# A gated cross-attention and feed-forward block on one core: the order of all five instruction streams is rewritten, the matmul stages run column by column, and the context chunks and weight sums change places

## The chip, the cores and the metric

The kernel runs on one core of a Trainium2 chip. The metric is the device time in microseconds (us) of one execution; lower is better. TensorE (PE) multiplies matrices, VectorE (DVE), ScalarE (ACT) and GpSimd (POOL) work on elements, and SyncE (SP) issues nearly all transfers (DMA). Each engine works through its own instructions in order and waits on semaphores where it needs another one's result.

## What is computed

```python
# x (2, 1024, 2048), ctx (2, 2048, 2048), weight (2048, 2048), all f32
def fake_quant(x, scale, zp):
    q = jnp.clip(jnp.round(x / s + z), 0, 255)
    return (q - z) * s
def xattn(x1, x2):                  # x1 = _layernorm(x), x2 = ctx
    return jnp.matmul(fake_quant(x1, ...), fake_quant(x2, ...))
def ffn(x, weight):                 # x = _layernorm(x)
    s = QP / jnp.clip(jnp.max(jnp.abs(x), axis=-1, keepdims=True), 1e-05, None)
    xq = jnp.clip(jnp.round(x * s), QN, QP) / s
    scale_w = 1.0 / jnp.clip(jnp.mean(jnp.abs(weight)), EPS, None)
    tw = jnp.clip(jnp.round(weight * scale_w), -1.0, 1.0)
    return jnp.einsum('bsi,oi->bso', xq, tw) / scale_w
x = x + jnp.tanh(g_xattn[0]) * xattn(_layernorm(x), ctx_4096)
x = x + jnp.tanh(g_ffn[0]) * ffn(_layernorm(x), weight)
```

Two things matter for the order. The feed-forward part needs the mean of all absolute weights before it can quantise the first one, so the weights are read twice. And each row of the first result must be complete before its layernorm and its largest value are known.

## The kernel before, in words

There are two batches `b` of 8 row tiles `m` (128 rows each) and 4 column chunks `c` (512 columns). A **unit** is one accumulator bank: one tile `m` times one chunk `c`, 16 matmuls of 128x512. TensorE does 128 units in four stages: X0 and X1 (cross-attention of batch 0 and 1), F0 and F1 (feed-forward of batch 0 and 1); stage X0 is units 0 to 31, X1 32 to 63, F0 64 to 95, F1 96 to 127. `UNITS` is their order. After a unit DVE adds it into the f32 rows `h` (`add`), which frees the bank (`acc_free`). X0 rotates over 8 banks, the later stages over 4, since the other 4 hold the halves that `halve` (ACT) writes and `max_h` (DVE) reduces to find each row's maximum.

Before a tile can be multiplied it goes through a chain: load x, statistics on DVE (`stats_x`), a square root on ACT (`deviation1`), `scale_x` on DVE, quantisation to int8 on POOL (`quant1`), a transposing transfer (`turn`, issued by SP), and a cast to bf16 into `lhs` (`lhs_bf`). `lhs` holds 8 tiles only, so a tile of the next stage can be cast when the last unit of the same `m` of this stage is done. `stats_h`, `scale_h`, `halve`, `max_h`, `peak_h`, `quant2` are the same chain for the feed-forward part.

A context chunk comes in 8 pieces of 512 KB: load, quantise to int8 (`ctx_quant`, mostly POOL), cast to bf16 (`ctx_bf`, ACT). Batch 0's pieces go through 8 slots (`stage`); batch 1's pieces and all weight halves go through `ring`, 4 slots of 512 KB, in the order of the table `RING` ("ctx" a piece of batch 1's context, "sum" a half weight tile for the mean, "quant" the same half again for quantisation). `q2` has two places for a bf16 chunk. Before, batch 0's chunks 2 and 3 are put into `upper`, the space of batch 1's tiles 4 to 7 in `h`. Later `q2` holds the ternary weights `tw`.

Everything is ordered by hand: the calls in each engine's function are that engine's order. SP's order also fixes the order of the transfers; a `turn` whose int8 tile is not ready holds up all loads behind it. `pace` lets a load start only when the one some three sizes before it has landed.

Of the kernel before, what the change touches and what calls it, by code (L numbers as in the profile page):

```python
# [5 lines left out]
def flamingo_gated_block(nc, x, ctx, g_xattn, g_ffn, s1, z1, s2, z2, weight, out):  # L6
# [8 lines left out]
    P = 128  # L15
# [13 lines left out]
    AHEAD = 3  # L29
# [28 lines left out]
    TURNS += [("h", 0, m) for m in A] + [("w", 0, t) for t in range(2 * TPC)]  # L58
    TURNS += [("h", 0, m) for m in Z] + [("w", 0, t) for t in range(2 * TPC, WT)] + [("h", 1, m) for m in range(M)]
# [22 lines left out]
    LN1 = [(0, m, m + 1) for m in range(M)] + [(1, 0, 4), (1, 4, 6), (1, 6, 8)]  # L82
    LN2 = [(b, h, h + NB) for b in range(B) for h in (0, NB)]
    LN2_VAR, LN2_OPS, PEAK_OPS = 2 * NB + 1, 2 * NB + 6, 4

    def ln1_count(g, whole):

        sizes = [m1 - m0 for _, m0, m1 in LN1]
        steps = [2 * n + 1 + (5 if n == 1 else 7) for n in sizes]
        return sum(steps[:g]) + (steps[g] if whole else 2 * sizes[g] + 1)  # L90

    def group_of(groups, b, m):
        return next(g for g, (gb, m0, m1) in enumerate(groups) if gb == b and m0 <= m < m1)
# [7 lines left out]
    with es:  # L101
# [16 lines left out]
        upper = h[:, 1, NB:M, :].rearrange("p m d -> p (m d)").bitcast(bf16).rearrange("p (c k n) -> p c k n", c=2, k=K)  # L118
# [3 lines left out]
        def chunk(b, c):  # L122
            return q2[:, c % 2, :, :] if b == 1 or c < 2 else upper[:, c - 2, :, :]
# [99 lines left out]
        def _(sp):  # L223
# [97 lines left out]
            for m in A[1:]:  # L321
                load_x(1, m)
# [663 lines left out]
```

## Time and profile before

| | us |
|---|---|
| median of 3 runs (lowest, highest) | 550.48 (550.24, 551.34) |
| the profiled execution | 551.01 |
| its span, first to last instruction | 549.2 |
| TensorE busy in the span | 466.0 |
| DVE, ACT, POOL busy | 255.2, 232.6, 160.9 |
| mean granted TensorE clock | 0.95 of full speed |
| read from memory, written | 83.89 MB, 16.78 MB |

The span is 1.8 us shorter than the time of the same execution. TensorE is the engine that is busy most; its idle time stands in a few places, so the way to read this profile is along TensorE's time line, asking at each gap what it waited for and what that in turn waited for.

### The profile page before, as it was taken

What the parts mean: (1) busy time and instruction counts of PE and PEld (TensorE: products, weight loads), DVE (VectorE), ACT (ScalarE), POOL (GpSimd) and SP (SyncE); (2) the same over time, 40 slices, a digit from 0 to 9 for tenths busy, and PEclk for the clock granted to TensorE, in tenths of its full rate; (3) what the DMA queues carried; (4) which work ended last, traced back from release to release, by engine and by line L of the source; (5) the groups of instructions that cost most, each with busy time, mean ns of one, the idle gap of its engine ahead of it and who ended that gap; (6) DMA issues with size and microseconds to landing.
All of it is one profiled execution on the core that took longest, in us unless ns stands there. A gap on an engine that the chain in (4) does not pass through costs nothing.

```text
span 549.2 us, 5796 instructions
## 1 busy us (share of the span) xinstructions
PE 466.0 (85%) x2027; PEld 202.2 (37%) x2048; DVE 255.2 (46%) x455; ACT 232.6 (42%) x235; POOL 160.9 (29%) x122
## 2 busy tenths in 40 slices
PE   0179968989994896759899779974999999999997
PEld 0024423434441342314344334431444444444443
DVE  4732152768107963793633374937932222222221
ACT  1266645221783567847974446238631410000000
POOL 2537653213962200177211471210431100000000
PEclk9999998999996898959999889996999999999999
DMA  7969968675999888788989998982180803030322
GB/s 243 261 199 338 326 205 287 187 222 205 267 366 344 226 251 294 245 280 200 333 263 268 272 208 229 305 230 81 76 222 9 229 1 154 0 154 0 154 76 76
DMA packets 88293, 113.78 MB, mean 207 GB/s; under 512 B 54720, under 2 KB 54720, under 8 KB 88256
## 3 DMA queue, kind: packets, MB, share of 16 engines
q1 hardware_dynamic: 87392, 113.27, 68.5%
q8 instruction: 25, 0.41, 0.3%
q10 hardware_dynamic: 864, 0.00, 0.1%
q14 instruction: 12, 0.10, 0.0%
HBM read 83.89 MB, written 16.78 MB: 183 GB/s over the span
## 4 chain that ended last, share of the span: by engine, by line
PE 31%; issue 30%; POOL 15%; DMA 12%; ACT 6%; DVE 3%; SPq 3%; POOLq 0%; ACTq 0%; DVEq 0%
PE acc L725 31%; POOL ctx_i L407 10%; DMA ring<-in_L_ffn_weight 5%; POOL tile_i L389 3%; DMA turned_i<-tile_i 3%; SPq L287 2%; DMA ctx_i<-tile_i 2%; ACT acc L521 1%; POOL tile_i L416 1%; ACT q L499 1%; DMA h<-in_ctx 1%; ACT ring L537 1%; DMA h<-in_x 1%; ACT q L554 1%; ACT tile_i L546 1%
## 5 line engine op out<-in xcount | busy, mean ns | idle before, releaser
L725 PE MATMUL acc<-q,lhs 128*128 128x512 fp8e4 x1024 | 226.6, 385 | 16.6 <-DVE h L851 11.0
L671 PE MATMUL acc<-q,lhs 128*128 128x512 bf16 x753 | 182.9, 400 | 56.2 <-DVE lhs L833 25.0
L851 DVE SCALAR_TENSOR_TENSOR h<-acc,smalls,h 128x512 f32<-128x512 f32 x128 | 93.8, 748 | 152.6 <-PE acc L725 121.3
L725 PEld LDWEIGHTS acc<-q,lhs 128*128 128x128 bf16 x1024 | 101.2, 99 | 142.0 <-DVE h L851 14.8
L671 PEld LDWEIGHTS acc<-q,lhs 128*128 128x128 bf16 x768 | 75.7, 101 | 162.4 <-issue 41.6
L389 POOL TENSOR_SCALAR tile_i<-h,smalls 128x2048 int8<-128x2048 f32 x32 | 68.4, 2141 | 120.5 <-DVE smalls L785 38.1
L760 DVE BATCH_NORM_STATS2 smalls<-h 128x6 f32<-128x512 f32 x64 | 39.8, 681 | 55.7 <-DMA h<-in_x 55.6
L671 PE MATMUL acc<-h,lhs 128*128 128x512 bf16 x250 | 57.5, 387 | 6.7 <-ACT h L499 6.4
L499 ACT ACTIVATE q<-ctx_i 128x1024 bf16<-128x1024 int8 x48 | 49.6, 1052 | 26.9 <-POOL ctx_i L407 26.0
L530 ACT ACTIVATE lhs<-turned_i 128x2048 bf16<-128x2048 int8 x20 | 37.9, 1902 | 46.7 <-DMA turned_i<-tile_i 46.7
L407 POOL TENSOR_SCALAR ctx_i<-ring,smalls 128x1024 int8<-128x1024 f32 x32 | 38.1, 1195 | 51.1 <-DMA ring<-in_ctx 48.7
L816 DVE TENSOR_REDUCE smalls<-acc 128x1 f32<-128x1024 f32 x32 | 37.7, 1220 | 18.9 <-ACT acc L521 18.7
L407 POOL TENSOR_SCALAR ctx_i<-h,smalls 128x1024 int8<-128x1024 f32 x28 | 33.4, 1195 | 26.4 <-DMA h<-in_ctx 25.6
L671 PEld LDWEIGHTS acc<-h,lhs 128*128 128x128 bf16 x256 | 25.3, 100 | 38.4 <-ACT h L499 7.3
L796 DVE BATCH_NORM_STATS2 smalls<-h 128x6 f32<-128x512 f32 x64 | 39.4, 679 | 0.0
L521 ACT ACTIVATE acc<-h,smalls 128x1024 f32<-128x1024 f32 x32 | 37.3, 1194 | 4.6 <-DVE smalls L816 4.6
L416 POOL TENSOR_SCALAR tile_i<-ring,smalls 128x1024 int8<-128x1024 f32 x16 | 18.9, 1182 | 59.0 <-DMA ring<-in_L_ffn_weight 51.2
L537 ACT ACTIVATE ring<-ring 128x1024 f32<-128x1024 f32 x32 | 33.4, 1045 | 6.2 <-DMA ring<-in_L_ffn_weight 6.1
L546 ACT ACTIVATE tile_i<-ring,smalls 128x1024 int8<-128x1024 f32 x16 | 18.1, 1144 | 33.8 <-DMA ring<-in_L_ffn_weight 33.6
L506 ACT ACTIVATE smalls<-smalls 128x1 f32<-128x1 f32 (+2 forms) x11 | 2.2, 200 | 49.1 <-DVE smalls L765 49.1
L499 ACT ACTIVATE h<-ctx_i 128x1024 bf16<-128x1024 int8 x16 | 16.8, 1054 | 8.5 <-POOL ctx_i L407 8.5
L530 ACT ACTIVATE lhs<-ctx_i 128x2048 bf16<-128x2048 int8 x8 | 15.1, 1902 | 4.2 <-DMA ctx_i<-tile_i 4.2
(57 smaller groups left out, 82.8 us busy)
## 6 DMA issues: line engine op xcount, KB each, us to landing
ring<-in_L_ffn_weight SPq DMA_DIRECT2D x64, 512.0 KB, 5.6
h<-in_ctx SPq DMA_DIRECT2D x32, 512.0 KB, 6.3
ring<-in_ctx SPq DMA_DIRECT2D x32, 512.0 KB, 6.0
h<-in_x SPq DMA_DIRECT2D x30, 512.0 KB, 6.6
out<-h SPq DMA_DIRECT2D x28, 512.0 KB, 2.6
out<-h SPq DMA_DIRECT2D x8, 256.0 KB, 2.4
h<-in_x SPq DMA_DIRECT2D x4, 256.0 KB, 5.0
turned_i<-tile_i SPq DMA_TRANSPOSE x32, 4.6
```

The source lines that it names most:

```text
L389: nc.gpsimd.tensor_scalar(tile_i8[:, n % TP, :], tile, scale, offset, ALU.mult, ALU.add).then_inc(i8_ready[n % TP], 1)
L407: nc.gpsimd.tensor_scalar(ctx_i8[:, piece % NB, :], src, inv_s[:, 1:2], dz[:, 1:2], ALU.mult, ALU.add).then_inc(used, 1)
L499: nc.scalar.activation(flat(chunk(b, c)[:, p * KP:(p + 1) * KP, :]), ctx_i8[:, piece % NB, :], ACT.Copy).then_inc(ctx_ready, 1)
L521: nc.scalar.activation(spare[:, cols], h[:, b, m, cols], ACT.Identity, bias=nb2[:, t:t + 1], scale=hr2[:, t:t + 1]).then_inc(half_ln, 1)
L530: nc.scalar.activation(in_pairs(lhs[:, m, :, :]), pairs_apart(n), ACT.Copy).then_inc(lhs_act, 1)
L537: nc.scalar.activation(half, half, ACT.Abs, accum_out=w_part[:, n:n + 1]).then_inc(ring_used[i % NB], 1)
L671: done = nc.tensor.matmul(acc, lhs[:, m, k, :], chunk(b, c)[:, k, :], start=(k == 0), stop=(k == K - 1))
L725: done = nc.tensor.matmul(psum[:, bank(u), :], lhs[:, m, k, :], tw[:, c, k, :], start=(k == 0), stop=(k == K - 1))
L760: ins = V.bn_stats(s[:, 6 * c:6 * c + 6], h[:, b, m, c * NC:(c + 1) * NC])
L796: ins = V.bn_stats(s[:, 6 * c:6 * c + 6], h[:, b, m, c * NC:(c + 1) * NC])
L816: V.tensor_reduce(amax[:, t, s:s + 1], spare[:, s * PW:(s + 1) * PW], AX.X, ALU.max, apply_absolute_value=True).then_inc(half_max, 1)
L851: V.scalar_tensor_tensor(out=hc, in0=psum[:, bank(u), :], scalar=gain, in1=hc, op0=ALU.mult, op1=ALU.add).then_inc(acc_free, 1)
```

## The change

- **Units.** X0 ran the upper four tiles (A) through all four chunks, then the lower four (Z). Now A and Z both run through chunks 0 to 2, and chunk 3 is done last for all eight tiles. X1, F0 and F1 ran in pairs of columns, half by half; now each column is done for all eight tiles before the next.
- **Places.** Batch 0's chunk 3 goes where chunk 0 was (`q2`), so `upper` holds one chunk and tiles 6 and 7 of batch 1 are free from the start. `chunk_before` names the column whose end a chunk has to wait for. The ternary weights of chunk `c` lie at `(c + 2) % C`.
- **Ring.** The weight sums stand between batch 1's context chunks; the last context chunk now comes after all sums.
- **Orders.** The call lists of SP, POOL, ACT, DVE and the opening of PE are all rewritten. A row tile's statistics of batch 1 are scaled one by one, those of the feed-forward part two by two (before in fours). Batch 1's tiles 0 to 3 are cast on DVE, no longer on ACT. The transposes of the feed-forward tiles 4 to 7 stand after the fourth weight tile's, no longer after the eighth's. `pace` allows one more load ahead after the first 24.

```diff
-    AHEAD = 3
-    OPENING = [(m, c) for c in range(C) for m in A]
-    OPENING += [(NB, c) for c in range(C)] + [(m, c) for c in range(C) for m in Z[1:]]
-    PAIRS = [(m, c) for pair in ((0, 1), (2, 3)) for half in (A, Z) for c in pair for m in half]
-    UNITS = [(X0, m, c) for m, c in OPENING] + [(s, m, c) for s in (X1, F0, F1) for m, c in PAIRS]
+    OPENING = [(m, c) for half in (A, Z) for c in range(C - 1) for m in half] + [(m, C - 1) for m in range(M)]
+    BY_COLUMN = [(m, c) for c in range(C) for m in range(M)]
+    UNITS = [(X0, m, c) for m, c in OPENING] + [(s, m, c) for s in (X1, F0, F1) for m, c in BY_COLUMN]
...
-    TURNS += [("h", 0, m) for m in A] + [("w", 0, t) for t in range(2 * TPC)]
-    TURNS += [("h", 0, m) for m in Z] + [("w", 0, t) for t in range(2 * TPC, WT)] + [("h", 1, m) for m in range(M)]
+    TURNS += [("h", 0, m) for m in A] + [("w", 0, t) for t in range(TPC)]
+    TURNS += [("h", 0, m) for m in Z] + [("w", 0, t) for t in range(TPC, WT)] + [("h", 1, m) for m in range(M)]
...
-        return (kind == "x" and b == 0 and m < NB) or (kind == "w" and m % 2 == 0)
+        return (kind == "x" and m < NB) or (kind == "w" and m % 2 == 0)
...
-    SUM_FIRST = 24
-    RING = [("ctx", i) for i in range(2 * PIECES)] + [("sum", i) for i in range(SUM_FIRST)]
-    RING += [("ctx", i) for i in range(2 * PIECES, C * PIECES)] + [("sum", i) for i in range(SUM_FIRST, 2 * WT)]
-    RING += [("quant", i) for i in range(2 * WT)]
+    RING = [("ctx", i) for i in range(PIECES)] + [("sum", n) for n in range(6)]
+    RING += [("ctx", i) for i in range(PIECES, 2 * PIECES)] + [("sum", n) for n in range(6, 20)]
+    RING += [("ctx", i) for i in range(2 * PIECES, 3 * PIECES)] + [("sum", n) for n in range(20, 2 * WT)]
+    RING += [("ctx", i) for i in range(3 * PIECES, C * PIECES)] + [("quant", n) for n in range(2 * WT)]
...
         def chunk(b, c):
-            return q2[:, c % 2, :, :] if b == 1 or c < 2 else upper[:, c - 2, :, :]
+            return q2[:, 1 - c % 2, :, :] if b else upper if c == 2 else q2[:, int(c == 1), :, :]
+
+        def chunk_before(b, c):
+
+            return {(0, 3): (X0, 0), (1, 0): (X0, 1), (1, 1): (X0, 3), (1, 2): (X1, 0), (1, 3): (X1, 1)}.get((b, c))
+
+        def ternary(c):
+            return tw[:, (c + 2) % C, :, :]
...
-                behind = 0
+                behind, far = 0, 3 if len(loads) < 24 else 4
...
-                    else:
-                        sp.wait_ge(acc_done, units_end(X0, c=2 + (m - NB) // 2))
+                    elif m < NB + 2:
+                        sp.wait_ge(acc_done, units_end(X0, c=2))
```

Three places show what the new orders do. First SP, in the stretch from the transposes of batch 1's tiles 4 to 7 to the last context chunk; before, it reads (`turned_i<-tile_i` is a transpose, `ring<-in_ctx` a context piece, `ring<-in_L_ffn_weight` a weight half, `h<-in_x` half an x tile):

```order
L246 DMA h<-in_x 128x1024 x4
L274 DMA ring<-in_L_ffn_weight 128x1024 x2
L287 DMA_TRANSPOSE turned_i<-tile_i 128x8x128 x2
L274 DMA ring<-in_L_ffn_weight 128x1024 x4
L287 DMA_TRANSPOSE turned_i<-tile_i 128x8x128
L274 DMA ring<-in_L_ffn_weight 128x1024 x2
L287 DMA_TRANSPOSE turned_i<-tile_i 128x8x128
L274 DMA ring<-in_L_ffn_weight 128x1024 x12
L268 DMA ring<-in_ctx 128x2x512 x16
```

The same stretch of SP in the changed kernel:

```order
L270 DMA ring<-in_ctx 128x2x512 x6
L286 DMA_TRANSPOSE turned_i<-tile_i 128x8x128
L270 DMA ring<-in_ctx 128x2x512
L273 DMA ring<-in_L_ffn_weight 128x1024 x3
L286 DMA_TRANSPOSE turned_i<-tile_i 128x8x128 x2
L273 DMA ring<-in_L_ffn_weight 128x1024 x4
L286 DMA_TRANSPOSE turned_i<-tile_i 128x8x128
L273 DMA ring<-in_L_ffn_weight 128x1024 x7
L270 DMA ring<-in_ctx 128x2x512 x8
L273 DMA ring<-in_L_ffn_weight 128x1024 x12
L270 DMA ring<-in_ctx 128x2x512 x3
```

The x loads are gone from here, the 16 context pieces in one run are split into 8 and 8, and the 12 sums that stood ahead of them or behind them now stand between.

Second DVE, at the casts of the last two ternary weight tiles of DVE (`q<-`), in F0. Before (`h<-acc,smalls,h` is an `add`):

```order
L798 BN_AGGR smalls<-smalls 128x2
L851 SCALAR_TENSOR_TENSOR h<-acc,smalls,h 128x512
L840 TENSOR_SCALAR q<-turned_i 128x16x128
L840 TENSOR_SCALAR q<-ctx_i 128x16x128
L803 TENSOR_SCALAR smalls<-smalls 128x4
L805 RECIPROCAL smalls<-smalls 128x4
```

The last of these two casts in the changed kernel, with what stands around it:

```order
L1057 SCALAR_TENSOR_TENSOR h<-acc,smalls,h 128x512
L1022 TENSOR_REDUCE smalls<-acc 128x1
L1046 TENSOR_SCALAR q<-ctx_i 128x16x128
L1057 SCALAR_TENSOR_TENSOR h<-acc,smalls,h 128x512
L1022 TENSOR_REDUCE smalls<-acc 128x1
```

Before, both casts stand together behind the add of unit 75; now the first stands behind that of unit 78 and the last behind that of unit 81, with adds and reductions between them.

Third ACT, in X1 from the square roots of batch 0's second layernorm on. Before (`q<-ctx_i` is `ctx_bf`, `acc<-h,smalls` half a tile's `halve`, `ring,smalls<-ring` a weight sum):

```order
L510 ACTIVATE smalls<-smalls 128x4
L537 ACTIVATE ring,smalls<-ring 128x1024 x2
L521 ACTIVATE acc<-h,smalls 128x1024 x2
L537 ACTIVATE ring,smalls<-ring 128x1024 x2
L521 ACTIVATE acc<-h,smalls 128x1024 x2
L537 ACTIVATE ring,smalls<-ring 128x1024 x2
L521 ACTIVATE acc<-h,smalls 128x1024 x2
L537 ACTIVATE ring,smalls<-ring 128x1024 x2
L521 ACTIVATE acc<-h,smalls 128x1024 x2
L499 ACTIVATE q<-ctx_i 128x1024 x8
```

The changed kernel, from the same point on:

```order
L615 ACTIVATE smalls<-smalls 128x2 x3
L604 ACTIVATE q<-ctx_i 128x1024 x2
L625 ACTIVATE acc<-h,smalls 128x1024
L604 ACTIVATE q<-ctx_i 128x1024 x2
L625 ACTIVATE acc<-h,smalls 128x1024
L604 ACTIVATE q<-ctx_i 128x1024 x3
L625 ACTIVATE acc<-h,smalls 128x1024
L641 ACTIVATE ring,smalls<-ring 128x1024 x4
L604 ACTIVATE q<-ctx_i 128x1024
L641 ACTIVATE ring,smalls<-ring 128x1024 x4
L625 ACTIVATE acc<-h,smalls 128x1024
```

Four whole tiles stood in one block between sums, ahead of all 8 casts of chunk 2; now the halves are spread among the casts of chunk 2 and the sums.

## Rows read from the trace of the kernel before

**Rows 1.** The page: span, TensorE's busy time, its granted clock in 40 slices.

```profile
span 549.2 us, 5796 instructions
...
PE 466.0 (85%) x2027; PEld 202.2 (37%) x2048; DVE 255.2 (46%) x455; ACT 232.6 (42%) x235; POOL 160.9 (29%) x122
...
PEclk9999998999996898959999889996999999999999
```

**Rows 2.** The waits of TensorE: waiter, releaser, total us, times, longest.

```profile
PE acc L671 <- DVE lhs L833: 25.0, 2, 18.2
PE acc L671 <- DVE h L851: 18.2, 9, 6.8
PE acc L725 <- DVE h L851: 11.0, 1, 11.0
PE acc L671 <- ACT q L499: 10.2, 12, 2.2
```

**Rows 3.** TensorE's time line: start, length, instructions, idle before and its releaser.

```profile
46.52 13.99 PE L671 MATMUL acc<-q,lhs 128*128 128x512 bf16 x63 [0.42 <-ACT q L499]
...
153.73 13.98 PE L671 MATMUL acc<-q,lhs 128*128 128x512 bf16 x62
174.52 9.78 PE L671 MATMUL acc<-q,lhs 128*128 128x512 bf16 x31 [6.82 <-DVE h L851]
...
305.06 15.66 PE L725 MATMUL acc<-q,lhs 128*128 128x512 fp8e4 x64 [2.79 <-ACT q L554]
323.53 43.20 PE L725 MATMUL acc<-q,lhs 128*128 128x512 fp8e4 x192 [2.81 <-ACT q L554]
377.76 167.72 PE L725 MATMUL acc<-q,lhs 128*128 128x512 fp8e4 x768 [11.04 <-DVE h L851]
```

**Rows 4.** DVE's time line at two of those gaps.

```profile
164.63 2.47 DVE L760 BATCH_NORM_STATS2 smalls<-h 128x6 f32<-128x512 f32 x4 [16.86 <-DMA h<-in_x]
...
278.16 0.21 DVE L865 TENSOR_SCALAR smalls<-smalls 128x1 f32<-128x1 f32 x1
...
368.09 1.29 DVE L840 TENSOR_SCALAR q<-ctx_i 128x2048 fp8e4<-128x2048 int8 x1 [6.36 <-DMA ctx_i<-tile_i]
```

**Rows 5.** SP's time line: runs of loads and some transposes.

```profile
36.67 24.84 SPq L255 DMA_DIRECT2D h<-in_ctx  x17
...
196.78 22.78 SPq L274 DMA_DIRECT2D ring<-in_L_ffn_weight  x12
222.51 30.70 SPq L268 DMA_DIRECT2D ring<-in_ctx  x16
...
273.33 3.78 SPq L274 DMA_DIRECT2D ring<-in_L_ffn_weight  x4
...
296.17 1.23 SPq L287 DMA_TRANSPOSE ctx_i<-tile_i  x1
...
314.16 1.35 SPq L287 DMA_TRANSPOSE ctx_i<-tile_i  x1
...
317.19 6.35 SPq L287 DMA_TRANSPOSE turned_i<-tile_i  x2
323.63 4.49 SPq L287 DMA_TRANSPOSE ctx_i<-tile_i  x2
...
359.63 1.25 SPq L274 DMA_DIRECT2D ring<-in_L_ffn_weight  x2
```

**Rows 6.** The page's DMA issues: count, size, median us to landing.

```profile
ring<-in_ctx SPq DMA_DIRECT2D x32, 512.0 KB, 6.0
...
turned_i<-tile_i SPq DMA_TRANSPOSE x32, 4.6
```

**Rows 7.** Groups by line and form: busy us, mean ns | idle before.

```profile
L407 POOL TENSOR_SCALAR ctx_i<-ring,smalls 128x1024 int8<-128x1024 f32 x32 | 38.1, 1195 | 51.1 <-DMA ring<-in_ctx 48.7 <-ACT q L499 1.5
...
L833 DVE CAST lhs<-turned_i 128x2048 bf16<-128x2048 int8 x4 | 5.1, 1275 | 7.0 <-DMA turned_i<-tile_i 6.9
...
L781 DVE SCALAR_TENSOR_TENSOR smalls<-smalls 128x1 f32<-128x1 f32 x8 | 1.8, 220 | 0.3
```

More of the change, by code:

```diff
@@ L233, in pace, with load_x0 @@
                 loads.append((landing, value, size))
+            def load_x0(first, end):
+                for c in range(first, end):
+                    pace(x0_in[c], 16, 0.5)
+                    sp.dma_start(h[:, 0, 0, c * NC:(c + 1) * NC], x_t[0][:, c * NC:(c + 1) * NC]).then_inc(x0_in[c], 16)
             def load_x(b, m):
@@ new lines, in _ @@
+            half_sum(6, 9)
+            lhs_bf(TURN_X[1, 5])
+            lhs_bf(TURN_X[1, 6])
+            half_sum(9, 13)
+            lhs_bf(TURN_X[1, 7])
+            half_sum(13, 17)
+            ctx_bf(47, 48)
+            half_sum(17, 20)
+            deviation2(0, 0)
+            deviation2(0, 2)
+            deviation2(0, 4)
+            ctx_bf(48, 50)
+            halve(0, 0, 0)
+            ctx_bf(50, 52)
+            halve(0, 0, 1)
+            ctx_bf(52, 55)
+            halve(0, 1, 0)
@@ new lines, in _ @@
+            half_sum(20, 24)
+            ctx_bf(55, 56)
+            half_sum(24, 28)
+            halve(0, 1, 1)
+            half_sum(28, 32)
+            halve(0, 2, 0)
+            halve(0, 2, 1)
+            deviation2(0, 6)
+            ctx_bf(56, 57)
+            halve(0, 3, 0)
+            ctx_bf(57, 59)
+            halve(0, 3, 1)
+            halve(0, 4, 0)
+            ctx_bf(59, 60)
+            halve(0, 4, 1)
+            ctx_bf(60, 62)
+            halve(0, 5, 0)
+            halve(0, 5, 1)
@@ L679, in pieces_ready, with opening @@
                 pe.wait_ge(ctx_ready, b * FIRST + c * PIECES + p + 1)
-            def opening(m, first, end):
+            def opening(m, c, first, end):
                 for p in range(first, end):
-                    pieces_ready(0, 0, p)
+                    pieces_ready(0, c, p)
                     if p == 0:
-                        begin(unit(X0, m, 0), TURN_X[0, m])
-                    xattn(0, m, 0, piece_of(p))
-            for p in range(4):
-                opening(0, p, p + 1)
-                opening(1, p, p + 1)
@@ new lines, in _ @@
+            opening(0, 3, 0, 8)
+            opening(1, 3, 0, 8)
+            opening(2, 3, 0, 8)
+            opening(3, 3, 0, 8)
+            opening(4, 3, 0, 8)
+            opening(5, 3, 0, 8)
+            opening(6, 3, 0, 8)
+            opening(7, 3, 0, 8)
+            for c in range(C):
+                for m in range(M):
+                    begin(unit(X1, m, c), TURN_X[1, m])
+                    for p in range(PIECES):
+                        if m == 0:
+                            pieces_ready(1, c, p)
+                        xattn(1, m, c, piece_of(p))
@@ L857, in weight_sum @@
                 for j in range(NB):
-                    dve.wait_ge(ring_used[j], RING_AT["quant", 0] // NB)
+                    i = max(i for i, (what, n) in enumerate(RING) if what == "sum" and i % NB == j)
+                    dve.wait_ge(ring_used[j], i // NB + 1)
                 step(n_w, w_steps, V.tensor_reduce(w_sum[:, :], w_part[:, :], AX.X, ALU.add))
```

1022 lines of the change are left out of this document (639 added, 383 removed).

## The prediction

> **What bounds the kernel now.** I read the page first. TensorE is busy for 466.0 of 549.2 us and its granted clock falls in several slices [rows 1]. The work itself is fixed: 2048 matmuls; a long undisturbed run of 768 takes 167.72 us, 0.2184 us each, so a unit of 16 costs 3.5 us, a stage of 32 units some 111 and a column of 8 units 27.8 [rows 3]. Then its waits [rows 2]: 25.0 us for the first tiles' casts at the start, 18.2 and 11.0 for banks that DVE frees, 10.2 for context casts. Then its time line, gap by gap [rows 3], and behind each gap the engine that released it.
>
> The start is a loading phase: the matmuls run without gaps from 46.5 on. X0 ends at 153.7. X1 should end 111 us later, at 265, and ends at 302.3 (305.06 - 2.79). One cause is the gap of 6.82: DVE stood 16.86 us before the statistics of a batch 1 tile [rows 4], because tiles 4 to 7 lie in `upper` and can't be loaded until X0's last columns are done, and the adds are queued behind them. Others are the four tiles that DVE reduces in one block, and chunk 2, whose place in `q2` comes free only 4 units before it is needed. F0 loses 2.79 and 2.81 to weights, then 11.04 because DVE stands before its last two weight casts (the last at 368.09) with the adds queued behind [rows 4]. After each of these gaps a run is too long for its count: 64 matmuls in 15.66 us are 1.7 over the 13.98 of a run at full clock (153.73). From 377.76 on nothing is lost; the last matmul ends at 545.5 and the span 3.7 later.
>
> **The change, stage by stage.** I follow the new orders with durations of the old trace.
>
> *Start and X0.* The first tile's cast moves behind the statistics of the fourth x tile, and POOL's quantisation of tile 1 behind a context piece, so the first matmul comes some 5 us later. That costs little: the fourth tile is cast at about the same time as before, since its load has the same bytes ahead of it, and the eight open banks let TensorE catch up. Then loads flow as in the run of 17 pieces in 24.84 us, 1.46 us each [rows 5]. Chunk 0 is complete on SP only after 14 pieces, no longer after 8, so I put its end on TensorE at 48; the 8 units of the upper tiles' chunks 1 and 2 take 28, 76, and 1 for single pieces: 77. Their last piece has the four lower x tiles (worth 8 pieces) and 10 pieces between it and chunk 0's last, which lands at some 44: 44 + 18 x 1.46 = 70, and is no hindrance. The lower tiles' casts hang on where SP issues their transposes: tile 7's stands behind pieces 24 to 31, the last issued at about 70 + 8 x 1.46 = 81, then 4.6 for the transpose [rows 6] and some 2 for the cast: 88. The same count gives 69, 77 and 83 for tiles 4 to 6, and the units need them at 77, 81, 85 and 93, in the order in which PE's opening is written. Chunk 3 needs column 0 to be done (about 97), takes 8 casts, and is ready by 107, needed at 118. So the remaining 20 units run on: 77 + 20 x 3.5 = 147. X0 gains about 7 us on 153.7.
>
> *X1.* Tiles 6 and 7 are loaded before 100, 4 and 5 at 118 (column 2 of X0 done), so DVE has its statistics well ahead: the 6.82 goes, with the 2.8 by which the run after it is too long (9.78 for some 32 matmuls of 0.218). Each chunk's place comes free a full column ahead instead of 4 units: that removes the 10.2 for context casts but for remnants. TensorE alone would end X1 at 147 + 111 = 258. What then comes last is the ring. Item 22 reuses the slot of a piece of chunk 1, and those wait for X0's end, so it goes out at about 150; 41 more must follow until the last context piece, which is now behind all sums. A ring item took 22.78 / 12 = 1.90 and 30.70 / 16 = 1.92 us in two runs of different kind [rows 5]. Both fit 4 slots that are each held for a landing of 6.0 and a conversion of 1.195 [rows 6, 7], (6.0 + 1.2) / 4 = 1.8. So 41 x 1.92 = 79, plus five transposes that SP issues in between at some 1.25 each and about 2 of waiting for them, 8: issued at 237, landed at 243, cast at 246. The seven tiles after the first follow: 246 + 7 x 3.5 = 270.5 for X1's end, 32 us earlier than now.
>
> *F0's start.* Before, the weight scale was known at 278.4 [rows 4] and F0 began at 305.06, 27 later, through quantising, transposing and casting four weight tiles. In the new order the sums are over before the last context chunk, so the scale is not waited for; the first weight half lands one ring item after the last context piece, at 245, and 245 + 2 for its neighbour + 27 = 274. That is a little later than X1's end, so F0 starts at 274 instead of 305.
>
> *Inside F0.* Now column 1's weights come after the transposes of tiles 4 to 7. From the fourth weight transpose (296.17) to the eighth (314.16) 18 us passed, and the four tile transposes took 317.19 to 328.1, 11 [rows 5]. From a fourth weight transpose to the stage that needs it are 305.06 - 296.17 = 9. So column 1 is ready 18 + 11 = 29 us after column 0, and needed 27.8 after: I charge 3 us, with the half clock after it. Columns 2 and 3 are 18 to 22 apart (32 halves in 87.5 us from 273.33 to 360.9 are 2.7 each [rows 5], 22 a column) and needed 27.8 apart: hidden. The last weight cast on DVE began at 368.09, 95 us after the first weight loads were issued at 273.33 [rows 4, 5]. Counted from 239, one ring item after the last context piece, this is 334; it stands before the add of unit 82 now, and TensorE can reach unit 86 without that add, at 274 + 22 x 3.5 = 351. The 11.04 goes.
>
> *More instructions.* Layernorm steps in pairs or singly instead of fours add some 64 small DVE operations, at up to 0.22 each about 14 us in all, and four casts of 1.275 move to DVE [rows 7], which is busy for 255.2 of 549.2 us [rows 1]. I cost them at nothing: they lie beside TensorE's units, of which each leaves DVE 3.5 us for an add. With that cover gone the most is 14 + 5 = 19; nothing is gained by them on DVE, and ACT is relieved of four casts.
>
> **Sum.** 274 (F0 starts) + 3 + 64 units x 3.5 = 223.6 + 3.7 (end) = 504.3. I add 4 for one more short gap with the lengthened run behind it, of the size that both edges of F0 show now, since no order of five queues fits everywhere: span 508. The profiled execution's time is 1.8 above its span, and the median 0.5 below that execution: 509.5.
>
> **A rule of the skill.** In the run of 17 pieces 512 KB took 1.46 us, which is 359 GB/s [rows 5]. The Trainium skill, "DMA: Bandwidth & Descriptors", section "Where 436 GB/s comes from", gives some 358 GB/s for a core as the memory side's limit; by that the trace agrees that this run was at the limit and the ring, at 273 GB/s, is not. If the limit and not the slots set the ring's pace, the sum would be that of the first rival.
>
> **Rivals.**
> - *The ring runs at the stage's rate* (more loads are let ahead, and slots are freed sooner by the spread order): 1.46 instead of 1.92, 42 x 0.46 = 19 earlier. Then TensorE itself is last, X1 ends at 258, F0 starts there: 258 + 3 + 223.6 + 3.7 = 488, 490 as a time. Against it: `pace` was not what the 1.92 fits, four slots are. 10%.
> - *The ring runs at 2.7 us an item*, as in the weight phase, because ACT and POOL now have halves, casts and quantisations between the ring's items and in-order engines hold slots: 42 x 0.78 = 33 later, 537 span, 539; with half of it 522. For it: ACT's new order has a halve behind every few ring items, and each waits for DVE's reduction. 22%.
> - *Slower than before.* One loop decides: DVE's adds 49 and 50 stand behind reductions whose halves stand on ACT behind sums 20 to 31, which wait for ring slots; POOL converts the last context pieces only behind quantisations that need those reductions. If each side waits for the other at most items, an item costs more than 1.92 + (549 - 508) / 42 = 2.90 us, and the kernel is slower than now. Nothing in the trace has an item that slow over 42 in a row: 4%.
> - *The order moves waits about and the sum stays*: 1% within 0.2%.
>
> The forecast, 496 to 520, has 63%. The range should leave out 2 in 10: it reaches down to 494, into the first rival, and up to 530, over the half-slow ring. 0.2%, about 1.1 us, is what a measurement of this kernel can tell from no change. Faster 0.95, same 0.01, slower 0.04.
>
> **What would show it.** Right: TensorE without a gap over 2 us from about 46 to 205; no wait of DVE for x over 5 us after 110; `ctx_bf` of the last chunk 1.9 us apart with POOL waiting for the ring; F0 starting within 5 us of X1's end, near 274; from there no gap over 3 us. Wrong: ring items over 2.3 us apart with the slot held by ACT or DVE; TensorE waiting for adds in X1; the lower tiles' transposes late on SP around 80 to 95, which would move everything behind by as much.

## The result and the profile after

The changed kernel takes 503.25 us (median of 4, 502.31 to 504.25) against 550.36 (549.05 to 551.34): a ratio of 0.915, with a 95% interval of 0.912 to 0.917. The forecast was 509.5, in a range of 494 to 530. In a second group of runs, on which the first comparisons below rest, the same kernel took 502.22, a ratio of 0.915 (0.908 to 0.923).

The page of the changed kernel, in answer to [rows 1]:

```profile
span 500.5 us, 5951 instructions
...
PE 450.2 (90%) x2048; PEld 200.3 (40%) x2048; DVE 290.2 (58%) x523; ACT 226.3 (45%) x241; POOL 163.4 (33%) x121
...
PEclk9999999999999999998599999999999999999999
```

Of the dents in the granted clock one is left, in slices 19 and 20 (225 to 250 us). TensorE's time line, in answer to [rows 3]:

```profile
28.82 7.41 PE L836 MATMUL acc<-q,lhs 128*128 128x512 bf16 x24 [28.82 <-ACT q L604]
37.73 8.79 PE L836 MATMUL acc<-q,lhs 128*128 128x512 bf16 x40 [1.50 <-DVE lhs L1039]
...
116.42 38.15 PE L836 MATMUL acc<-q,lhs 128*128 128x512 bf16 x176
...
171.78 58.87 PE L836 MATMUL acc<-q,lhs 128*128 128x512 bf16 x272 [0.69 <-ACT lhs L634]
234.14 2.62 PE L836 MATMUL acc<-q,lhs 128*128 128x512 bf16 x6 [3.49 <-DVE h L1057]
241.93 1.03 PE L836 MATMUL acc<-q,lhs 128*128 128x512 bf16 x2 [5.17 <-ACT q L604]
244.00 1.98 PE L836 MATMUL acc<-q,lhs 128*128 128x512 bf16 x4 [1.04 <-ACT q L604]
248.16 26.82 PE L836 MATMUL acc<-q,lhs 128*128 128x512 bf16 x116 [2.17 <-ACT q L604]
275.61 221.17 PE L942 MATMUL acc<-q,lhs 128*128 128x512 fp8e4 x1024 [0.63 <-DVE h L1057]
```

X0's last 8 units begin at 116.4 and end 27.7 later, at 144.1. F0 and F1 are one line: 1024 matmuls in 221.17 us without a gap. The whole saving can be laid along three stretches:

| stretch of the span | before | after | saved |
|---|---|---|---|
| start to the end of X0 | 153.7 | 144.1 | 9.6 |
| X1 with what follows it, to F0's start | 151.3 | 131.5 | 19.8 |
| F0's start to the last matmul | 240.4 | 221.2 | 19.2 |

The last matmul's distance to the end, 3.7, is the same. What still costs time is one place: 11.9 us in four gaps between 230.6 and 248.2. The table of windows shows it and the clock around it (length of the window; busy times of PE, PEld, DVE, ACT and POOL; then granted clock, the DMA engines' share and GB/s):

```profile
205.00:222.00 17.00, 17.00 (x80) 7.74 (x79) 6.64 (x12) 13.55 (x22) 6.47 (x4) 1.00 0.92 278
222.00:242.00 20.00, 11.35 (x48) 4.52 (x46) 7.60 (x19) 6.40 (x7) 4.02 (x5) 0.81 0.39 126
242.00:275.00 33.00, 29.77 (x122) 11.86 (x122) 28.93 (x42) 26.51 (x21) 17.95 (x12) 0.86 1.07 271
275.00:497.00 222.00, 221.17 (x1024) 100.12 (x1024) 100.30 (x154) 65.69 (x51) 34.81 (x22) 1.00 0.50 148
```

From 222 to 242 TensorE, ACT and POOL are busy for a smaller share than in the window above, and the DMA share falls to 0.39, so neither bandwidth nor a busy engine explains it. POOL's time line does:

```profile
222.68 1.22 POOL L471 TENSOR_SCALAR ctx_i<-ring,smalls 128x1024 int8<-128x1024 f32 x1 [0.78 <-DMA ring<-in_ctx]
232.26 0.40 POOL L501 PARTITION_ALL_REDUCE smalls<-smalls  x1 [8.36 <-issue]
239.60 3.54 POOL L471 TENSOR_SCALAR ctx_i<-ring,smalls 128x1024 int8<-128x1024 f32 x3 [6.94 <-issue]
```

The all-reduce that adds the weight sums over the partitions takes 0.40 us. But POOL does nothing for 8.36 us ahead of it and 6.94 behind it, and the releaser is "issue": it waited for nothing that the profile shows. From 223.9 to 239.6 POOL converts no context piece. Around it ACT waits 13.60 for the next piece (`240.82 ... ACT L604`), DVE 7.87 for the scale, with the adds behind, and SP needs 18.63 us for the last four context pieces, since their slots aren't freed. The prediction did not have this.

### The profile page after: what moved, and what is told of

Read it like the earlier page. It is cut to its first block, busy times and chain, and to the rows that moved or that the text cites. A ratio compares the mean times of both kernels' runs of the same rounds, so it can differ in the third digit from the quotient of the medians.

```text
span 500.5 us, 5951 instructions
## 1 busy us (share of the span) xinstructions
PE 450.2 (90%) x2048; PEld 200.3 (40%) x2048; DVE 290.2 (58%) x523; ACT 226.3 (45%) x241; POOL 163.4 (33%) x121
## 4 chain that ended last, share of the span: by engine, by line
PE 67%; issue 15%; POOL 6%; DMA 4%; ACT 4%; DVE 2%; SPq 1%; POOLq 0%; ACTq 0%; DVEq 0%
PE acc L942 44%; PE acc L836 22%; POOL ctx_i L471 5%; DMA h<-in_ctx 3%; ACT q L604 2%; DMA h<-in_x 2%; POOL tile_i L453 1%; DVE q L1046 1%; DVE smalls L1000 0%; ACT acc L625 0%; DVE h L1057 0%; SPq L236 0%; DVE smalls L992 0%; ACT L610 0%; ACT L582 0%
## 5 line engine op out<-in xcount | busy, mean ns | idle before, releaser
L836 PE MATMUL acc<-q,lhs 128*128 128x512 bf16 x896 | 201.8, 387 | 45.9 <-ACT q L604 37.8
L942 PE MATMUL acc<-q,lhs 128*128 128x512 fp8e4 x1024 | 221.2, 379 | 0.6 <-DVE h L1057 0.6
L836 PEld LDWEIGHTS acc<-q,lhs 128*128 128x128 bf16 x896 | 87.7, 99 | 159.2 <-ACT q L604 43.5
L942 PEld LDWEIGHTS acc<-q,lhs 128*128 128x128 bf16 x1024 | 100.1, 98 | 121.7 <-DVE h L1057 1.1
L604 ACT ACTIVATE q<-ctx_i 128x1024 bf16<-128x1024 int8 x56 | 56.7, 1047 | 50.1 <-POOL ctx_i L471 39.6
L471 POOL TENSOR_SCALAR ctx_i<-ring,smalls 128x1024 int8<-128x1024 f32 x32 | 40.1, 1256 | 41.9 <-DMA ring<-in_ctx 33.6
L634 ACT ACTIVATE lhs<-turned_i 128x2048 bf16<-128x2048 int8 x16 | 30.2, 1901 | 37.1 <-PE acc L942 24.9
L836 PE MATMUL acc<-h,lhs 128*128 128x512 bf16 x128 | 28.0, 379 | 0.0
L836 PEld LDWEIGHTS acc<-h,lhs 128*128 128x128 bf16 x128 | 12.5, 98 | 15.1
L1039 DVE CAST lhs<-turned_i 128x2048 bf16<-128x2048 int8 x8 | 11.4, 1430 | 4.9 <-DMA turned_i<-tile_i 4.7
L604 ACT ACTIVATE h<-ctx_i 128x1024 bf16<-128x1024 int8 x8 | 8.4, 1052 | 5.7 <-POOL ctx_i L471 5.4
```

The costliest lines, as they stand in the source:

```text
L471: nc.gpsimd.tensor_scalar(ctx_i8[:, piece % NB, :], src, inv_s[:, 1:2], dz[:, 1:2], ALU.mult, ALU.add).then_inc(used, 1)
L604: nc.scalar.activation(flat(chunk(b, c)[:, p * KP:(p + 1) * KP, :]), ctx_i8[:, piece % NB, :], ACT.Copy).then_inc(ctx_ready, 1)
L634: nc.scalar.activation(in_pairs(lhs[:, m, :, :]), pairs_apart(n), ACT.Copy).then_inc(lhs_act, 1)
L836: done = nc.tensor.matmul(acc, lhs[:, m, k, :], chunk(b, c)[:, k, :], start=(k == 0), stop=(k == K - 1))
L942: done = nc.tensor.matmul(psum[:, bank(u), :], lhs[:, m, k, :], ternary(c)[:, k, :], start=(k == 0), stop=(k == K - 1))
```

## The experiments

Twelve kernels ran, in three groups of four; each group is compared with the kernel before on the same chip (549.3, 550.3 and 550.9 us). `one` is a column of ones. The first four are about POOL's stall; the first of them is the changed kernel again, with no edit.

> The changed kernel once more, as the ruler for the three runs beside it on the same chip. Both theories: 502 to 505 us; TensorE stands four times between 230 and 250 us, 11 to 12 us in all, and POOL does nothing that the profile shows for 8 us before and 7 us after its sum over the partitions.

**Measured:** 502.22 us, span 500.3. The result repeats, with four gaps of together 12.1 us and F0's start at 275.39.

**The sum over the partitions on TensorE** in place of POOL:

```diff
-            weights_over_partitions()
...
+                    if unit(X1, m, c) == 55:
+                        pe.wait_ge(w_steps, 1)
...
+                        nc.tensor.matmul(psum[:, bank(55), 0:1], one[:, :].to_broadcast([P, P]), w_sum[:, :],
+                                         start=True, stop=True).then_inc(w_all_done, 1)
+                        pe.wait_ge(w_steps, 2)
```

(The memset of `one` and the wait for it are left out here. TensorE goes on when DVE has read the sum, and `weight_scale` stands ahead of one reduction more in DVE's order.)

> The sum of the weight sums over the partitions is made by one small f32 matmul on TensorE, ahead of unit 55, instead of POOL's sum over the partitions. Theory S (the switch of POOL to that operation and back, some 15 us, holds the last five context pieces): POOL converts the last context pieces without a break, the four gaps of TensorE near 240 shrink from 12 us to 1 to 3, F0 starts at 262 to 267 instead of 275.6, and the time is 489 to 494 us. Theory R (the ring and its loads would have held the last context pieces anyway): the last context piece lands at the same time, 501 to 504 us.

**Measured:** 490.47 us (490.27 to 492.93), ratio 0.894 (0.887 to 0.902), span 488.5. TensorE's time line of this kernel from the new matmul on:

```profile
225.20 0.28 PE L929 MATMUL acc<-smalls 128*128 128x1 f32 x2
225.73 5.35 PE L833 MATMUL acc<-q,lhs 128*128 128x512 bf16 x24 [0.25 <-DVE smalls L1073]
231.80 0.60 PE L833 MATMUL acc<-q,lhs 128*128 128x512 bf16 x2 [0.71 <-ACT q L601]
...
235.95 27.77 PE L833 MATMUL acc<-q,lhs 128*128 128x512 bf16 x116 [2.60 <-ACT q L601]
263.56 221.18 PE L945 MATMUL acc<-q,lhs 128*128 128x512 fp8e4 x1024
```

The sum is there in 0.28 us, 3.9 us of gaps are left of 11.9 (one of 0.34 is not in the rows), and F0 starts at 263.56 instead of 275.61: those 12.05 us are the whole difference of the two spans. This version beats both kernels.

**The all-reduce late**, behind the last context piece on POOL (the scale in DVE's order behind it), the computation otherwise as in the changed kernel:

```diff
-            ctx_quant(56, 59)
-            weights_over_partitions()
-            ctx_quant(59, 62)
+            ctx_quant(56, 62)
             quant2(0, 2)
             ctx_quant(62, 64)
+            weights_over_partitions()
```

> POOL's sum over the partitions stays, but stands behind the last context piece, and DVE's scale of the weights behind the add of unit 56. Theory S: the context gaps go (last context cast near 240 instead of 249), but the scale is known near 250 instead of 233 and the weights of F0's first column are late: F0 starts at 272 to 280 with a wait for weights or adds ahead of it, 499 to 508 us. Theory R: nothing gained at the context pieces, and the late scale costs up to 10 us: 505 to 513.

**Measured:** 503.69 us (501.85 to 505.07). The stall moves with the instruction and costs as much at F0's start:

```profile
243.85 0.40 POOL L501 PARTITION_ALL_REDUCE smalls<-smalls  x1 [8.76 <-issue]
251.57 2.04 POOL L453 TENSOR_SCALAR tile_i<-h,smalls 128x2048 int8<-128x2048 f32 x1 [7.32 <-issue]
```

The context gaps shrink to 1.85 and 0.57, and TensorE waits 11.15 us for F0's first weights instead (`274.54 ... PE L941 ... [11.15 <-ACT q L655]`).

**A second all-reduce early**, to have its first use out of the way where POOL has time (its result is not used):

```diff
-            ctx_quant(25, 34)
+            ctx_quant(25, 28)
+            step([9], nc.gpsimd.partition_all_reduce(dz_all[:, :], dz[:, 0:1], P, bass.bass_isa.ReduceOp.add))
+            ctx_quant(28, 34)
```

> One more sum over the partitions, of a constant nobody reads, on POOL near 79 us, where it stands idle for 17 us; the real one stays where it is. If the 15 us are paid once for the first use, they fall into that idle time, the real one costs under 2 us and the time is 489 to 495 us. If they are paid at every change of POOL between this operation and the others, both have them, X0's chunk 3 keeps its time and the time stays at 502 to 505 us.

**Measured:** 503.09 us (501.0 to 504.39). POOL's time line at both:

```profile
83.33 0.40 POOL L523 PARTITION_ALL_REDUCE smalls<-smalls  x1 [5.81 <-issue]
...
233.09 0.40 POOL L502 PARTITION_ALL_REDUCE smalls<-smalls  x1 [8.65 <-issue]
240.44 3.56 POOL L472 TENSOR_SCALAR ctx_i<-ring,smalls 128x1024 int8<-128x1024 f32 x3 [6.95 <-issue]
```

The second use pays as much as a lone one. So this is no cost of the first use in a program. It shows at every all-reduce of these kernels, on the way to it and again on the way back, on each side where POOL had tensor operations to do. Two all-reduces in a row were not run, so a cost of the change and a cost of each use are not told apart. The Trainium skill, "GPSIMD Engine Reference", section "2.1 Instruction dispatch", states some 6 us for the first call of a freshly loaded kernel, "with no visible profile instruction". The size and the invisibility agree with the early one (5.81). If "first" is read as once in a program, it does not hold here: the second one has 8.65 us ahead of it.

**The next four** undo or repair one part each. First the 11.04 us gap in F0 of the kernel before, which the prediction put down to the casts on DVE:

```diff
-            weight_fp8(12)
-            weight_fp8(14)
             scale_h(1, NB)
             for m in A:
                 max_h(1, m)
                 add(76 + m, 77 + m)
             peak_h(1, 0)
+            weight_fp8(12)
+            weight_fp8(14)
```

> The kernel before, with DVE's last two weight casts behind the first four maxima and adds of the feed-forward batch 1 instead of ahead of them. The prediction says that the 11.04 in F0 stands there because adds are queued on DVE behind casts whose weights are not there yet. If so, the gap before unit 84 goes with the lengthened run behind it, and the time falls from 549 to about 537. Rival: the weights themselves are late for TensorE, so that the gap only moves on by a few units: 545 to 550. A gap of 11 that stays where it is would say that neither the casts nor the weights made it.

**Measured:** 551.9 us, ratio 1.001 (0.997 to 1.005): nothing. Its profiled execution (span 552.6, the slowest of the ten) still has the gap, 10.24 before 380.19, and DVE now stands somewhere else:

```profile
361.66 0.16 DVE L803 TENSOR_SCALAR smalls<-smalls 128x4 f32<-128x4 f32 x1
376.02 0.18 DVE L805 RECIPROCAL smalls<-smalls 128x4 f32<-128x4 f32 x1 [14.20 <-ACT smalls L510]
...
379.39 0.74 DVE L851 SCALAR_TENSOR_TENSOR h<-acc,smalls,h 128x512 f32<-128x512 f32 x1
```

The reciprocal waits 14.20 for a square root on ACT, and ACT takes it only behind its own casts of the last weight tiles (367.09 and 373.91), which are late too. The casts on DVE were one of two waits that end together, since both hang on the same late weights. My first theory of this gap fell; a later run (below) tests its repaired form.

**The sums last**: the changed kernel with the last 8 weight sums behind the last context chunk, as before the change.

```diff
-    RING += [("ctx", i) for i in range(2 * PIECES, 3 * PIECES)] + [("sum", n) for n in range(20, 2 * WT)]
-    RING += [("ctx", i) for i in range(3 * PIECES, C * PIECES)] + [("quant", n) for n in range(2 * WT)]
+    RING += [("ctx", i) for i in range(2 * PIECES, 3 * PIECES)] + [("sum", n) for n in range(20, 24)]
+    RING += [("ctx", i) for i in range(3 * PIECES, C * PIECES)] + [("sum", n) for n in range(24, 2 * WT)]
```

(With them ACT's last 8 sums move behind its last context casts, POOL's all-reduce behind the last context piece, and DVE's sum and scale behind the add of unit 56.)

> The changed kernel, with the last 8 weight sums behind the last context chunk again, and the sum over the partitions and the scale behind them. The prediction's reason for sums between the context chunks is that the scale is then not waited for, at the price of a later last context piece. Its working gives: last context piece 8 items of 1.85 = 15 earlier, so X1 is not held by context and ends near 258; last sum issued at 222 + 15 and landed at 243 at the latest, sum over partitions behind POOL's stall of 8.4 at some 249, scale at 251, F0 27 later at 278, two later than now: 503 to 507. Rival A (the scale was never what F0 waited for): F0 starts with X1's end at 258 to 262 and the time is 487 to 491. Rival B: POOL's two stalls of together 15 us now stand fully in the path of the first weights: F0 at 285 or later, 512 or more.

**Measured:** 504.38 us (503.64 to 505.22), ratio 0.917 (0.911 to 0.923). TensorE waits 5.03 for adds and 11.10 for weights; F0 starts at 275.60, to a hundredth where it starts in the changed kernel. POOL's rows:

```profile
242.59 0.41 POOL L502 PARTITION_ALL_REDUCE smalls<-smalls  x1 [15.67 <-DVE smalls L1065]
253.00 2.04 POOL L454 TENSOR_SCALAR tile_i<-h,smalls 128x2048 int8<-128x2048 f32 x1 [10.00 <-issue]
```

The way there is hidden in POOL's wait for the sums, the way back (10.00) is not. With the all-reduce in the program, the place of the sums is worth some 2 us at most (504.4 against 502.2 and 503.3, and 502.4 for the next kernel, which ran beside it).

**One load less ahead**: `behind, far = 0, 3` throughout instead of 4 after the first 24 loads.

> The changed kernel, with loads let ahead by 3 everywhere instead of 4 after the first 24. The ring ran at 1.85 us an item from the 22nd to the 59th, where 1.92 was predicted from four slots. If slots bind, one load less ahead changes nothing: 501 to 504.5, and items at 1.85. Rival: the further load is what made the ring faster, then items are at 1.92 or slower, 38 items x 0.07 or more = at least 3 us later at the last context piece and up to 3 us on the time: 505 or more.

**Measured:** 502.36 us (500.51 to 502.94), ratio 0.913 (0.908 to 0.917), span 500.8. Nothing: items 22 to 59 go out 1.83 us apart, against 1.85 in the changed kernel. `pace` was not what set the ring's rate, as the prediction had said.

**The start as before**: the order of the first loads, casts and quantisations (tiles 0 to 3, up to the second transpose) from the kernel before, with the rest of the changed one, so a mixture of the two.

```diff
             load_x(0, 1)
+            load_first(0, 1)
             load_x(0, 2)
-            load_x(0, 3)
-            load_first(0, 2)
             turn(TURN_X[0, 0])
+            load_first(1, 2)
+            load_x(0, 3)
             load_first(2, 5)
```

(and on DVE `lhs_bf` of tile 0 ahead of the statistics of tile 2 and that of tile 1 ahead of the statistics of tile 3, and two swaps on POOL and ACT.)

> The changed kernel, with the order of loads, casts and quantisations of the first four tiles as before. The first matmul comes some 4.5 us earlier (24 instead of 28.8). The prediction says that the late start costs little, since TensorE catches up against the loads: X0 then ends within 1 us of 144.1 and the time stays at 501 to 505. Rival: the 4.5 us go through to the end of X0 (139.6), the ring's batch 1 pieces go out as much earlier, and the time falls to 498 to 499.

**Measured:** 514.43 us (512.03 to 519.14), ratio 0.937 (0.932 to 0.943), 11 to 12 slower than the changed kernel. Neither number was expected. TensorE's and DVE's time lines of this kernel:

```profile
18.31 1.01 PE L837 MATMUL acc<-q,lhs 128*128 128x512 bf16 x2 [18.31 <-DVE lhs L1040]
...
36.62 5.54 PE L837 MATMUL acc<-q,lhs 128*128 128x512 bf16 x14 [8.51 <-ACT q L605]
```

```profile
31.28 1.23 DVE L1040 CAST lhs<-turned_i 128x2048 bf16<-128x2048 int8 x1 [8.79 <-DMA turned_i<-tile_i]
32.43 2.47 DVE L979 BATCH_NORM_STATS2 smalls<-h 128x6 f32<-128x512 f32 x4
```

The first matmul comes 10.5 us earlier, and X0 ends at 153.5, 9.4 later. DVE stands 8.79 before the cast of tile 1, whose transpose SP issues behind five context loads; the statistics of tile 3 are queued behind that cast. POOL waits 9.62 us for their scale (until 36.93), with the next context pieces queued behind, and tile 3 is cast at 43.12 instead of 37.75. So an earlier first matmul does not make X0 end earlier. What held this kernel is when the last of the four tiles and the pieces are there; the new order puts all loads and statistics of the four tiles ahead of the first cast. The run does not weigh the old start as such: in the kernel before, the transpose of tile 1 goes out at 20.01, ahead of those context loads, and tile 1 is cast at 24.40. From X0's end on, TensorE's rows stand 9 to 11 later than in the changed kernel.

**The last four.** The small matmul in the kernel before, in place of its all-reduce (before unit 57; the edit is that of the second kernel):

> The kernel before, with the sum over the partitions made by one small matmul on TensorE (before unit 57) instead of POOL's all-reduce. Theory: in the kernel before, POOL's first stall lies in its 13.00 of waiting for the sums and costs nothing, and only the second (7.56 between the all-reduce and the first weight quantisation) is in a path, of which at most 2.8 shows at F0's start, 2.8 at the next gap and a part of the 11.0 behind. So between 538 and 548, much less than the 12 us that the same edit gives the changed kernel, or nearly as much if all three gaps shrink. Rival: ring loads and not POOL pace the first weights, then nothing changes: 549 to 551.

**Measured:** 547.45 us (545.32 to 551.02), ratio 0.993 (0.989 to 0.996). The edit that is worth 12 us in the changed kernel is worth some 3 here (2 to 6 by the interval): F0 begins at 303.92 with a gap of 0.19 instead of 2.79, and the gap before the third line stays, 11.26. In the kernel before, POOL waited for the sums anyway ahead of the all-reduce, and behind it the first weight quantisation now comes 3.5 us earlier, at 281.71.

**Adds first**: the kernel before, with DVE's adds of units 76 to 79 ahead of both waits, and so every later add four units ahead too.

```diff
+            add(76, 77)
             weight_fp8(12)
+            add(77, 78)
             weight_fp8(14)
+            add(78, 80)
             scale_h(1, NB)
             for m in A:
                 max_h(1, m)
-                add(76 + m, 77 + m)
+                add(80 + m, 81 + m)
```

> The kernel before, with DVE's adds of units 76 to 79 ahead of the two last weight casts, of the wait for ACT's square root and of the first maxima (everything behind them four adds further on). The move of the casts alone changed nothing, since DVE then stood 14.20 before that square root, which ACT takes behind its own casts of the same late weights. If the gap before unit 80 is made by adds queued behind either wait, it goes now with the lengthened run behind it: 549 to about 537. Rival: column 2's or 3's weights themselves are late for TensorE, then a gap of 5 or more comes at unit 80 or 81 with a cast as its releaser: 544 to 549.

**Measured:** 535.36 us (534.5 to 536.84), ratio 0.971 (0.964 to 0.978). From the second line of F0 on TensorE has no gap left in this kernel:

```profile
303.80 13.97 PE L725 MATMUL acc<-q,lhs 128*128 128x512 fp8e4 x64 [2.85 <-ACT q L554]
321.61 207.36 PE L725 MATMUL acc<-q,lhs 128*128 128x512 fp8e4 x960 [3.84 <-DVE h L851]
```

The repaired theory holds: the gap was made by adds queued on DVE behind waits, not by late weights. Adds moved ahead by four units give some 15 of the 47 us, and most of the 19.2 that the whole change saves in F0 and F1.

**Both**: sums last, and the sum over the partitions on TensorE (before unit 60).

> The changed kernel with both edits: the last 8 weight sums behind the last context chunk, and the sum over the partitions on TensorE (before unit 60). With the all-reduce, sums last and sums between gave the same time, each held by POOL: sums between lost 12 us of context pieces, sums last lost 10.00 behind the all-reduce. If sums between context chunks are worth something once POOL doesn't stand, F0 starts 275.6 - 9.5 = 266 here against 263.6 with sums between: 492 to 496. Rival A: no difference, 490 to 491.5. Rival B: the late sums hold the scale to 250 or so, F0 at 270 or later: 497 or more.

**Measured:** 498.12 us (495.42 to 498.71), ratio 0.901 (0.895 to 0.908). F0 starts at 269.25 behind a gap of 3.54 for weights, 5.7 later than with the sums between; the scale is known at 244.7 here and at 226.1 there. The four combinations:

| | sums between | sums last |
|---|---|---|
| all-reduce on POOL | 502.2 | 504.4 |
| matmul on TensorE | 490.5 | 498.1 |

The table's kernels ran in different groups. Where POOL doesn't stand, sums between context chunks are worth 7.6 us by these medians and some 4 by the two ratios, whose intervals overlap in part; the eight runs don't overlap. Part of it is DVE's order and not the ring's: DVE waits 9.04 us for the last sums with reductions and adds queued behind, and TensorE waits 4.72 for an add (at 252.65). Another place for the sum and the scale in DVE's order was not run.

**Three slots** of the ring instead of four, up to the last context piece, in the version with the matmul:

```diff
+    SLOT = [i % 3 if i < 64 else (i + 1) % 4 for i in range(len(RING))]
+    NTH = [SLOT[:i].count(SLOT[i]) for i in range(len(RING))]
```

> The version with the sum on TensorE, with only 3 of the ring's 4 slots in use up to the last context piece (all 4 behind it). If slots set the ring's pace as the prediction says, an item costs (6.0 + 1.2) / 3 = 2.4 us instead of the 1.8 measured, 41 items are 24 later, and the time is 508 to 515. Rival: transfers at the memory's or the pacing rule's rate set it, then a slot less changes little: 490 to 494. Landing times that shrink as fewer loads are in flight would give something between.

**Measured:** 519.46 us (517.83 to 519.67), 29 slower than with four. SP's time line at item 22, at the 12 weight sums ahead of the last context chunk and behind them: with four slots, then with three:

```profile
149.65 2.68 SPq L274 DMA_DIRECT2D ring<-in_L_ffn_weight  x3
...
189.56 19.33 SPq L274 DMA_DIRECT2D ring<-in_L_ffn_weight  x12
211.72 3.69 SPq L271 DMA_DIRECT2D ring<-in_ctx  x3
```

```profile
160.53 8.06 SPq L276 DMA_DIRECT2D ring<-in_L_ffn_weight  x3
...
213.90 24.99 SPq L276 DMA_DIRECT2D ring<-in_L_ffn_weight  x12
240.15 4.58 SPq L273 DMA_DIRECT2D ring<-in_ctx  x3
```

From the first sum to the item behind the twelfth, an item takes 22.16 / 12 = 1.85 us with four slots and 26.25 / 12 = 2.19 with three. Times the slots, each is held 7.4 and 6.6 us, and the median landing of these 12 is 5.8 and 5.0: the hold follows the landing, as (landing + conversion) / slots has it, and slots bind, not the memory's rate. The last context piece goes out at 257.5 instead of 225.3. Of these 32 us 11 are there at item 22 already (160.5 for 149.65), and 21 come over the 41 items behind it (97 us for 75.6).

## Why the prediction was right, and where it was not

**Start and X0: right.** The first matmul came at 28.8 (forecast some 23), the upper tiles' 12 units ended at 75 (77), SP had issued the lower tiles' last transpose by 78 (81), and X0 ended at 144.1 (147) without a gap from 47 on but for 0.38. That the late first matmul costs little held: in the mixture, which starts 10.5 earlier, X0 ended 9.4 later. Which part of the 9.6 saved is owed to the start and which to the new order of units was not separated.

**X1: the two waits went.** The 6.82 for x is gone, and in X1 up to 230 so are the waits for context casts; no wait of DVE that ends between 110 and 230 reaches 5 us. What is left of gaps up to 230 is 0.93, 1.45 and 0.69. Behind 230 TensorE waits 8.4 for context casts once more, and that is the all-reduce.

**X1's end: right by errors against each other, so luck in the number.** The forecast was 270.5, measured 275.0. The last context piece was to go out at 150 + 79 + 8 = 237. The version without the stall shows this sum by itself: item 22 goes out at 149.65, as forecast, and the last piece at 225.3, 12 earlier than forecast. The 41 items took 75.6 us, 1.84 each, the five transposes among them included. So most of the error is the term "8" for the transposes, put on top of the items: slots come free while SP issues them, and the items behind go out closer together. In the changed kernel seven sums follow the third of them in 8.88:

```profile
163.95 1.36 SPq L286 DMA_TRANSPOSE turned_i<-tile_i  x1
166.74 8.88 SPq L273 DMA_DIRECT2D ring<-in_L_ffn_weight  x7
176.20 14.11 SPq L270 DMA_DIRECT2D ring<-in_ctx  x8
191.08 19.08 SPq L273 DMA_DIRECT2D ring<-in_L_ffn_weight  x12
213.29 4.54 SPq L270 DMA_DIRECT2D ring<-in_ctx  x3
...
222.72 18.63 SPq L270 DMA_DIRECT2D ring<-in_ctx  x4
```

The rest of the 12, some 3, is the item itself, 1.84 for 1.92. Behind the last piece X1's end was put 33.5 us later and came 38.3 later (263.6), which takes 5 of the 12 back. The all-reduce then adds 11.4 and makes it 275.0.

The mechanism, (landing + conversion) / slots, was right, as three slots show. What the prediction divided was a run's own length (22.78 / 12), which leaves out SP's wait before the item that follows. From start to start the 12 sums took 25.73 / 12 = 2.14 before (196.78 to 222.51 in [rows 5]) and take 22.21 / 12 = 1.85 now (191.08 to 213.29). Times four slots, each was held 8.6 and is held 7.4, though their median landing rose from 5.7 to 6.2: what is left beside the landing fell from 2.9 to 1.2, and 1.05 of it is ACT's own operation. Behind two sums in a row, ACT did this in the kernel before:

```profile
214.75 2.32 ACT L521 ACTIVATE acc<-h,smalls 128x1024 f32<-128x1024 f32 x2
```

and this behind four in the changed one:

```profile
209.71 1.19 ACT L625 ACTIVATE acc<-h,smalls 128x1024 f32<-128x1024 f32 x1
```

A landed item waited for ACT through twice as much, twice as often. That this is the whole of the 1.7 us between 2.9 and 1.2 is argued, no run took it apart. I had taken the rate from a stretch in which the old order was at work, and the change is one of orders.

The other error was the all-reduce, which the list of moved work did not hold at all: 15.3 us of idle POOL around it, moved from a place where POOL waited anyway into the middle of the last context pieces. The row at 222.72 above is this gap. The matmul in its place shows the size: 12 us. Rows of the old trace that I had not read had shown it:

```profile
277.21 0.40 POOL L460 PARTITION_ALL_REDUCE smalls<-smalls  x1 [13.00 <-DVE smalls L859]
285.18 2.21 POOL L416 TENSOR_SCALAR tile_i<-ring,smalls 128x1024 int8<-128x1024 f32 x2 [7.56 <-issue]
```

The way to the all-reduce lies in the 13.00 of waiting, the way back stands open, 7.56.

**F0's start: 275.6 for 274, with the chain of the first weights sized right.** The forecast had the weights last, 3.5 behind X1's end: first half landed at 245, F0 29 later. Measured, that half landed at 248.1, and ACT's last cast of column 0 ended 27.3 later:

```profile
273.44 1.91 ACT L656 ACTIVATE q<-ctx_i 128x2048 fp8e4<-128x2048 int8 x1 [4.81 <-DMA ctx_i<-tile_i]
```

Its end, 275.35, X1's end, 275.0, and the add that TensorE waited for (gap 0.63), 275.4, lie within half a us. So it was a tie, and the weights alone were not what F0 waited for; in the version without the stall TensorE's own end came last (263.6, with the last such cast over at 262.3). "The scale is not waited for" was right: it was known at 233.3, 15 us before the first half landed. That sums between the context chunks gain something by this shows only where the all-reduce is gone, as 5.7 at F0's start.

**Inside F0: better than forecast.** The 3 us charged for column 1's weights and the 4 for one more short gap did not come; both stages ran at full clock, 221.2 for 223.6. The 11.04 went, as said, but the reason was half of it: the casts on DVE were one of two waits, and without them the other was as long. Adds ahead of both is what removes it, and in the changed kernel the last two weight casts stand between adds (at 328.27 and 340.48), with no wait of 5 us at either.

**More instructions: nothing, as forecast, though their size was not.** DVE is busy 35 us longer, 290.2 for 255.2, where I had put 19 as the most. Some 24 of the 35 are the small operations, put at 14: several take longer than 0.22 (those of line 988 have a mean of 633 ns over 16, the same step before, line 773, 356 ns over 8). No run tests why. And yet TensorE waited for it only 3.5 us behind the all-reduce, 0.6 at F0's edge and 2.4 for casts. The sum, 508 for the span, becomes 500.5 by +1.6 at F0's start and -3, -2.4 and -4 behind it.

**The rivals.** "The ring runs at the stage's rate" said 490, and without the stall the kernel takes 490.5, but not for its reason: an item took 1.84 and not 1.46, slots set the pace and not more loads ahead, and X1 ends 5 later and the rest earlier than it had them. The ring at 2.7 an item and the slower-than-before loop did not form. The 359 GB/s of the prediction come from the same division as its items: from its first issue to the next load behind it (62.77) a piece of the 17 took 1.54 us, and the DMA engines of the kernel before moved 310 GB/s in that stretch (36.7 to 61.5), and 291 and 249 in the ring's two. The ring was the slower one all the same.

## What to carry to other kernels

When a change reorders engines, list each moved instruction with the idle time on both sides of it, "issue" above all: work that is cheap by its duration can carry a changeover that was hidden in its old place. A queue's rate taken from a run of the old order holds that order's delays; count it from start to start, split it into landing and the rest of the hold, ask what the new order puts between, and don't add on top what is issued while the queue waits anyway. And a gap that ends with one late release may have a second wait of the same length beside it, so test it by moving what is queued behind, not what stands in front.

## What the runs showed of the hardware

- `partition_all_reduce` of 128x1 shows 0.40 us, with 5.8 to 8.8 us of idle POOL ahead of it and 6.9 to 10.0 behind it wherever POOL had work waiting on that side; in a program with two of them, the second had 8.65 ahead of it and 6.95 behind.
- A matmul of f32 128x128 by 128x1, its stationary side a column of ones read with step zero, adds 128 partitions in two records of together 0.28 to 0.38 us and leaves the sum in every partition.
- Landing of a 512 KB load shrank with the loads in flight: a median of 6.0 us over batch 1's context pieces with four slots, 5.3 with three.
- A transposing transfer took a median of 6.0 us in the changed kernel and 4.6 in the one before [rows 6], with the same sizes; nothing here tests why.
